# Cross-attention and FFN layer on one core: query projections of two head groups in one PSUM bank, every second slot

## The reference

```python
h = layernorm(x)
q, k, v = h @ wq + bq, ctx @ wk + bk, ctx @ wv + bv          # 16 heads of 32
score = (q @ k.T) / sqrt(32) * mask;  score = where(score == 0, -1e9, score)
x1 = x + (softmax(score) @ v) @ wo + bo
out = x1 + real(ifft(fft(layernorm(x1)) @ (wr + i wi))) + bias
```

## Time and profile before

| | before |
|---|---|
| median of 3 runs | 458.8 us (458.41 to 458.97) |
| span of the profiled execution | 457.1 us (the page gives no time of its own for it) |
| busy PE, PEld | 442.1 (97%), 293.3 (64%) |
| busy DVE, ACT, POOL | 398.0 (87%), 372.6 (82%), 359.6 (79%) |
| chain that ended last | PE 79%, DVE 10%, issue 5%, ACT 3%, DMA 1% |
| mean granted clock of PE | 0.996 |

### The profile page before, as it was taken

The page is one execution under the profiler, slowest core; times in us unless marked ns, Lnnn a source line. Parts: engine busy times, 40 slices in busy tenths (PEclk is TensorE's granted clock), DMA queues, the critical chain, the costliest instruction groups (busy, mean ns, idle before and its releaser), DMA issues.

```text
span 457.1 us, 11172 instructions
## 1 busy us (share of the span) xinstructions
PE 442.1 (97%) x3510; PEld 293.3 (64%) x3510; DVE 398.0 (87%) x630; ACT 372.6 (82%) x1434; POOL 359.6 (79%) x540
## 2 busy tenths in 40 slices
PE   6989898999999999999999999999999999999997
PEld 5777686777666666666666666666666666555444
DVE  3797699899999999999999999999999898999443
ACT  3358597789999999898989898989989888899720
POOL 6588744795889899998989898869899685976663
PEclk9999998999999999999999999999999999999999
DMA  8996752332445454545555445445433334330344
GB/s 288 392 368 182 236 195 71 97 86 71 90 92 142 122 147 115 152 110 143 128 134 138 116 107 148 91 114 147 115 96 70 97 74 98 70 93 13 82 104 126
DMA packets 85287, 60.16 MB, mean 132 GB/s; under 512 B 40141, under 2 KB 72813, under 8 KB 84718
## 3 DMA queue, kind: packets, MB, share of 16 engines
q1 hardware_dynamic: 84508, 59.29, 47.3%
q10 hardware_dynamic: 722, 0.17, 0.2%
HBM read 29.33 MB, written 8.39 MB: 83 GB/s over the span
## 4 chain that ended last, share of the span: by engine, by line
PE 79%; DVE 10%; issue 5%; ACT 3%; DMA 1%; ACTq 0%; POOL 0%; DVEq 0%
PE bank L438 32%; PE bank L525 17%; PE bank L582 10%; PE bank L599 6%; PE scores L570 5%; PE bank L443 4%; DVE zs L867 3%; PE bank L595 3%; DVE zs L860 1%; ACT zs L688 1%; DMA bqb<-in_bq 1%; PE scores L443 1%; DVE cn L883 1%; ACT pt L697 1%; DVE x L845 1%
## 5 line engine op out<-in xcount | busy, mean ns | idle before, releaser
L688 ACT ACTIVATE zs<-zs,nbias 128x128 f32<-128x128 f32 x512 | 199.6, 397 | 8.2 <-POOL nbias L1093 7.9
L688 ACT ACTIVATION_READ_ACCUMULATOR zs<-zs,nbias 128x1 f32 x512 | 99.4, 194 | 0.0
L867 DVE SCALAR_TENSOR_TENSOR zs<-zs 128x1024 f32<-128x1024 f32 x64 | 81.3, 1270 | 0.2
L872 DVE TENSOR_REDUCE nmin<-zs 128x8 f32<-128x1024 f32 x64 | 78.1, 1220 | 2.2
L860 DVE TENSOR_TENSOR zs<-scores,ms 128x1024 f32<-128x1024 f32 x64 | 78.0, 1218 | 0.3 <-issue 0.3
L525 PE MATMUL bank<-xth,wqh 128*128 128x256 f16 x256 | 70.9, 277 | 4.0 <-DVE kl L810 2.0
L697 ACT COPY pt<-bank 128x512 f32<-128x512 f32 x128 | 68.4, 586 | 6.7 <-PE bank L582 6.3
L525 PE MATMUL bank<-xtl,wqh 128*128 128x256 f16 x256 | 70.4, 275 | 0.0
L525 PE MATMUL bank<-xth,wql 128*128 128x256 f16 x256 | 70.4, 275 | 0.0
L582 PE MATMUL bank<-ident,zs 128*128 128x128 f32 x512 | 67.5, 275 | 0.7 <-ACT zs L688 0.7
L1053 POOL TENSOR_TENSOR xs<-xs,bob 128x512 f32<-128x512 f32 (+1 forms) x41 | 42.4, 1036 | 24.5 <-DVE zs L867 24.5
(11 more groups left out here) (118 smaller groups left out, 960.1 us busy)
## 6 DMA issues: line engine op xcount, KB each, us to landing
xs<-in_x SPq DMA_DIRECT2D x16, 512.0 KB, 4.2
xtr<-in_xt SPq DMA_DIRECT2D x16, 512.0 KB, 4.4
out<-x SPq DMA_DIRECT2D x31, 256.0 KB, 2.6
qs<-qh SPq DMA_DIRECT2D x120, 64.0 KB
lp<-in_lparts SPq DMA_DIRECT2D x4, 1024.0 KB, 9.0
qs<-ql SPq DMA_DIRECT2D x60, 64.0 KB
ms<-in_mask SPq DMA_DIRECT2D x16, 128.0 KB, 2.6
wqs<-in_wq SPq DMA_DIRECT2D x2, 512.0 KB, 6.8
```

The lines of the kernel that those rows point to most:

```text
L688: last = act.activation(z, z, ACT.Exp, bias=nbias[:, s % 4, i:i + 1], scale=-NEG, accum_out=zsum[:, s % 4, i:i + 1])
L867: dve.scalar_tensor_tensor(out=z, in0=z, scalar=0.0, in1=z, op0=ALU.is_equal, op1=ALU.subtract).then_inc(eq_done, 1)
L872: dve.tensor_reduce(nmin[:, s % 4, :], zs[:, s % NZ].rearrange("p t h k -> p (t h) k"), AX.X, ALU.min).then_inc(mn_done, 1)
```

## The change

Two head groups' projections become one fill `QQ(c, i)`, i = 0 or 1: 24 matmuls of 256 columns, the first 12 into the lower half of a bank, the next 12 into the upper half. It stands in odd slots only: `QQ(c, 0)` in slot 4c-9, `QQ(c, 1)` in slot 4c-7, where `Q(c, 0)` to `Q(c, 3)` stood in slots 4c-9 to 4c-6. Slots 2 to 6 have a new table. ACT and DVE take out 512 columns with one instruction each. The rows of statistics get a fill of their own, `ST(c)`, late in slot 4(c-2) for c = 3 to 15; it was part of `Q(c-1, 2)` before, three slots earlier (by the old table, slot 3 for c = 3). The waits for "the last projection of a chunk" (SP's `stack_q` and last transposes, ACT's `split_hi`) name `QQ(c, 1)`. Chunks 0 and 1 keep `Q`.

```diff
-    queries = {2: [(2, 0), (2, 1)], 3: [(2, 2)], 4: [(2, 3), (3, 0)], 5: [(3, 1)], 6: [(3, 2), (3, 3)]}
+    queries = {2: (2, 0), 4: (2, 1), 5: (3, 0), 6: (3, 1)}
...
-        late = [("Q",) + f for f in queries.get(v, [divmod(v + 9, 4)]) if f[0] < NC]
+        late = []
+        if v % 4 == 0 and 3 <= v // 4 + 2 < NC:
+            late.append(("ST", v // 4 + 2))
+        if v in queries:
+            late.append(("QQ",) + queries[v])
+        elif v >= 7 and v % 2 == 1 and (v + 9) // 4 < NC:
+            late.append(("QQ", (v + 9) // 4, (v + 9) % 4 // 2))
...
+        def last_query(c):
+            return at["Q", c, 3] if c < 2 else at["QQ", c, 1]
...
             def stack_q(c):
-                sp.wait_ge(g_free, at["Q", c, 3] + 1)
+                sp.wait_ge(g_free, last_query(c) + 1)
...
-                    if f == 2 and 3 <= c + 1 < NC:
-                        last = stat_rows(o, c + 1)
+                elif kind == "QQ":
+
+                    pe.wait_ge(p_l1, c)
+                    for i in range(2):
+                        g = slice(256 * f + 128 * i, 256 * f + 128 * i + 128)
+                        mm = []
+                        for k in range(4):
+                            mm += [(wqh[:, k, g], xth[:, c % 2, k]), (wql[:, k, g], xth[:, c % 2, k]),
+                                   (wqh[:, k, g], xtl[:, c % 2, k])]
+                        last = full_mm(o[:, 256 * i:256 * i + 256], mm)
...
-                    last = act.copy(qh[:, c % 2, f, :], src[:, 0:256])
+                    last = act.copy(qh[:, c % 2, 2 * f:2 * f + 2, :], src[:].rearrange("p (g n) -> p g n", g=2))
...
             def split_hi(c):
                 act.wait_ge(d_xt[c % NT], 16 * (c // NT + 1))
                 if c >= 2:
-                    act.wait_ge(g_done, at["Q", c - 2, 3] + 1)
+                    act.wait_ge(g_done, last_query(c - 2) + 1)
...
+                elif kind == "QQ":
+                    g = slice(2 * f, 2 * f + 2)
+                    last = dve.tensor_tensor(ql[:, c % 2, g, :], src[:].rearrange("p (g n) -> p g n", g=2),
+                                             qh[:, c % 2, g, :], ALU.subtract)
```

More of the change, by code:

```diff
@@ L254, in build @@
         for n, f in enumerate(fills):
-            if f[0] in ("Q", "U", "M", "K", "W1", "Z"):
+            if f[0] in ("Q", "QQ", "U", "M", "K", "W1", "Z"):
                 hi_count[n] = len(hi_count) + 1
+        def last_query(c):
+            return at["Q", c, 3] if c < 2 else at["QQ", c, 1]
         def tile_of(c, t):
@@ L345, in turn_x1n @@
                 if c == NC - 1:
-                    sp.wait_ge(g_done, at["Q", c, 3] + 1)
+                    sp.wait_ge(g_done, last_query(c) + 1)
                     sp.wait_ge(h2_done, n + 1)
@@ L524, in fill @@
                     for i, (a, b) in enumerate(mm):
[L525 to L529, removed]
-                    if f == 2 and 3 <= c + 1 < NC:
-                        last = stat_rows(o, c + 1)
+                        pe.matmul(o[:, 0:256], a, b, start=(i == 0), stop=False)
+                    pe.wait_ge(wz_lo, f // 2 + 1)
+                    pe.wait_ge(st_done, c + 1)
+                    last = pe.matmul(o[:, 0:256], wz[:, g], srow[:, c], start=False, stop=True)
+                elif kind == "QQ":
[7 more added lines that the diff above has]
+                        last = full_mm(o[:, 256 * i:256 * i + 256], mm)
                 elif kind == "WO":
@@ L655, in hi @@
                 elif kind == "Q":
-                    if f == 2 and 3 <= c + 1 < NC:
-                        stat_copy(src, c + 1).then_inc(st_done, 1)
+                    last = act.copy(qh[:, c % 2, f, :], src[:, 0:256])
+                elif kind == "QQ":
                     if f == 0 and c == 2:
```

## The result

| | before | with the change |
|---|---|---|
| median | 458.8 us (458.41 to 458.97, 5 runs) | 460.23 us (459.97 to 460.70, 5 runs) |
| ratio, 95% interval | | 1.0034 (1.0021 to 1.0046) |
| span of the profiled execution | 457.1 us | 458.7 us (its own time 460.46) |
| busy PE, DVE, ACT, POOL | 442.1, 398.0, 372.6, 359.6 us | 442.1, 395.7, 372.7, 365.5 us |

The kernel became slower by 1.4 us. PE's busy time is the same to 0.1 us; DVE, which lost 28 instructions as ACT did, has 2.3 us less work; neither says where the time went. The start of each slot on PE (the first of the eight transposes) says it. Where the changed kernel has done one more half projection than the old one, 1.31 us of work is subtracted.

What follows compares the result with a forecast made beforehand. PE's own instruction list was taken to bound the middle, with engines taking turns in head and tail. Middle +0.6, head -0.1 and tail +0.3 gave +0.8 us: 457.9 in the profile, 459.6 as median, range 457.3 to 462.3 (forecast's own 458.5 to 460.8).

Steps and rivals of the forecast that it cites:

- What bounds the middle: Slots 13 to 54: PE's own instruction list sets the time; no new wait, thinnest cover 1.3 us at the bank.
- The rival of a new wait in the middle: Slots with r = 1: bank of `QQ` freed too late, 0.5 us 11 times, +5.5 us, 465; chance 0.15.
- What ACT and DVE save is worth nothing: Middle: about 0.15 us a pair saved on each engine, hidden behind PE and costed at nothing.
- Products with V, then transposes, 0.05 us each: Middle, behind even slots: transposes take 0.92 us in place of 0.87 to 0.88, at 22 places.
- The places behind `ST`, taken at half: Middle: at 11 of 22 places `ST` stands between; cost between 0 and 0.05 us more, half taken.
- The 0.01 us saved by a pair: Middle: 24 matmuls in a row have one start fewer, 0.2 us less over 21 pairs.
- The tail, +0.3 us: From slot 54: late transposes delay DVE's subtraction and `mask_mul(56)`; +0.3 us, from 0 to 1.3.
- The sentence that from there DVE sets the pace: Tail, from `mask_mul(56)` at about 382.8: DVE bounds, 5.36 us to the next against PE's slot of 4.85.
- The head, -0.1 us: Slots 3 to 13: PE's lead and later waits net -0.1 us, ends -2.4 and +1.3.
- the sentence that PE would be 0.7 us ahead by slot 12: Head: PE about 0.7 us ahead by slot 12, counted in work done.
- the head's rival: Head and tail: clock stays at 2.4 GHz, slot 12's wait is filled; head -2.4 us, 457.3; chance 0.20.
- The prediction's 1.7 us for the low clock in the kernel before: Head, around slot 5: slower matmuls cost 1.2 us over 12 and about 0.5 behind them.

Runs made afterwards that it cites:

- split_out: Changed kernel with each pair taken out by two 256-column instructions on ACT and two on DVE in place of one of 512; 460.67 us, ratio 1.0036.
- scores_between: Changed kernel with the next step's scores directly behind the products with V in slots 14, 18, ... 54; 459.88 us, ratio 1.0026.
- head_single: Changed kernel with chunks 2 to 4 on single projections in the old slots and rows, pairs from chunk 5 on; 459.27 us, ratio 1.0009.
- pair_in_10: Changed kernel with the pair of chunk 4's second half in slot 10 in place of slot 9; 459.32 us, ratio 1.0015.
- best: Changed kernel with chunks 2 to 4 and 15 single, old table, next scores behind products with V in slots 14, 18, ... 54; 458.45 us, ratio 0.9999.
- early_pairs: Changed kernel with pairs in slots 2, 3, 4 and 6 in place of 2, 4, 5 and 6; 462.51 us, ratio 1.0083.
- all_three: Changed kernel with pairs in slots 2, 3, 4, 6, chunk 4's second pair in slot 10, and scores behind products with V; 460.56 us, ratio 1.0043.
- rows_alone: Kernel before with only the rows of statistics made a fill of their own, late in slot 4(c-2), single projections kept; 466.06 us, ratio 1.0147.

## Why the prediction was right, and where not

- **What bounds the middle**: right. PE is full and waits for no one in slots 16 to 54 (the earlier trace rows and their counterpart above); the bank, the scores, the chain over ACT's late copies all kept their cover. The rival of a new wait in the middle did not occur, and `split_out`, which lengthens that very chain, cost nothing there.
- **What ACT and DVE save is worth nothing**: right, shown by `split_out` (221.90 against 221.91 us).
- **Products with V, then transposes, 0.05 us each**: right in cause and size, shown by `scores_between`. The places behind `ST`, taken at half, cost next to nothing in the transposes (0.88 against 0.87), `ST` itself 0.12 us in place of 0.11. The 0.01 us saved by a pair is there too (2.63 us against twice 1.32). Counted alike the middle measured +0.4 us for 36 slots, predicted +0.6 for 42. Why the transposes take longer behind the products with V is argued from the loads alone. The Trainium skill (TensorE: Matmul & The Clock Gate, Step-by-step: what each phase is for) has PE pull a load ahead of matmuls in flight when the row groups don't conflict or the load goes to the background buffer. Whether either holds here no run shows, so the prediction went too far when it took from this rule that the loads would hide in either order. In the trace the load behind a pair starts 0.11 us ahead of its transposes, behind the products with V not at all (250.60 and 255.51 above).
- **The tail, +0.3 us**: right in size, in part by luck. The subtraction for slot 54 came 1.5 us later relative to slot 55 and `mask_mul(56)` 0.25 us, as predicted, but no wait of PE follows from that: 0.06 us is again the order of two products, and 0.16 us a wait for POOL, whose scalings took 1.82 in place of 1.67 us. The sentence that from there DVE sets the pace is the one that these rows don't bear out.
- **The head, -0.1 us**: wrong, measured +0.8 in the profile and 1.0 in the medians of the change and `head_single`. The step that failed is the sentence that PE would be 0.7 us ahead by slot 12: counted in work done it was 1.0 us behind (114.67 less 1.31, before 112.32). I had DVE's slots 10 and 11 0.6 us late, because ACT waits for transposes behind the pair of slot 9 (that wait is in the trace: 1.22 us at 103.20), but I did not set this against PE's own shortened slot 10. PE passed it in 3.94 us and met `mask_mul` at the scores of slot 11, 1.37 us too early. `pair_in_10` takes this meeting away and 0.9 us with it. The 0.4 us I had for the bank in slot 13 were there (0.27 and 0.11), and so was the wait for the stacked queries.
- **The clock in slot 5**: I left it open; it stayed at 2.4 GHz in this execution. The length of PE's wait alone does not decide it. `scores_between` waited 1.29 us in slot 5 like the changed kernel, and its clock fell (0.57 from 69.5 to 73.5 us); `head_single` and `best` waited 1.60 and 1.59 us, as the kernel before did, and theirs stayed at 1.00. What decides it is open. Nor does the clock at 70 us decide between the forecast and the head's rival, as I had written: it was 1.00, and the head was slower than both. The full clock did not bring the gain of the head's rival: in `scores_between` 24 matmuls took 4.29 us in place of 2.63, and slot 7's wait for the DMA vanished in return. Slot 8 began at 87.29 there, at 86.75 with the change, so 1.2 of the 1.7 us came back two slots later. The prediction's 1.7 us for the low clock in the kernel before is too large in the same way: `best`, with the same order up to slot 8 and full clock, starts slot 8 only 0.5 us earlier, and then PE waits 0.87 us in slot 6, at the product that needs DVE's folds.

The sum of +0.8 us was half of the 1.6 in the profile; what it lacked is the head. That left the median 0.6 us above the forecast and inside the forecast's own range. There was some luck in it: the five runs of the change all had the full clock, while the kernel before was profiled with the low one. Against the executions of the kernel before with the full clock (median 458.6) the change costs 1.7 us: 1.0 in the head, 0.4 in the middle, 0.25 in the tail.

## What to carry to other kernels

Where one engine is full, count only its own list, and read what each neighbour in that list costs from start to start: an order of two products was worth more here than 28 instructions on each of two other engines. When work is gathered into every second slot, check each meeting in the shortened slots too, and most of all in the head, where the full engine of later is not yet the late one. An extra fill in a ring of banks was free under a full producer and cost microseconds under a late consumer; there a larger fill that takes one place in the ring for two was the cheaper form. And before a gain is read from two profiles, compare their mean clocks and a stretch in which their orders are the same.

## What was not expected of the hardware

- With a gap of some 3 us on PE in the head the mean clock falls in some executions and not in others: in `early_pairs` runs with a mean clock of 0.993 take 2.7 us longer than those with 0.999 and more (median 463.86 against 461.12). The two kernels with this gap spread the most, 460.8 to 464.0 us (`early_pairs`) and 459.2 to 462.1 (`all_three`), six runs each; `best` spreads from 458.2 to 459.1. In `rows_alone`, where PE waits 3.74 us, all four runs had the lower clock. No profile of a slower execution of `early_pairs` was kept, so that the gap is the cause is argued.
- The kernel before drew the lower clock (0.995 or 0.996) in 11 of the 60 executions beside these experiments. They took 458.9 to 460.7 us, median 459.1; the others took 458.2 to 459.3, median 458.6. That is as much as the smaller effects of this study; spans are compared best between executions of the same mean clock.
